# Relative values of an attention kernel: four query shifts with both halves of the table as weights, instead of eight shifts and three products

## The reference

```python
rel_pos = jnp.arange(L)[None, :] - jnp.arange(L)[:, None] + (MAX_LEN - 1)
rel_v = relative_v[rel_pos]                      # (L, L, 16): a row of the table for each pair
scores = jnp.einsum('bhld,bhrd->bhlr', Q, K) * scale + jnp.einsum('bhld,lrd->bhlr', Q, rel_k)
attn = jax.nn.softmax(scores, axis=-1)
out = jnp.einsum('bhlr,bhrd->bhld', attn, V) + jnp.einsum('bhlr,lrd->bhld', attn, rel_v)
```

## Time and profile before

| | us |
|---|---|
| median of three runs | 3464.99 (3463.78 to 3466.43) |
| span of the profiled execution, first to last instruction | 3463.7 |
| attention stage, about | 180 to 2890 |
| TensorE matmuls busy | 3194.2 (92%) |
| TensorE weight loads busy | 2524.8 (73%) |
| VectorE busy | 2813.3 (81%) |
| ScalarE busy | 2634.6 (76%) |
| GpSimd busy | 2262.5 (65%) |

### The profile page before, as it was taken

The page is one execution under the profiler, slowest core; times in us unless marked ns, Lnnn a source line. Parts: engine busy times, 40 slices in busy tenths (PEclk is TensorE's granted clock), DMA queues, the critical chain, the costliest instruction groups (busy, mean ns, idle before and its releaser), DMA issues. The chain is left out here.

```text
span 3463.7 us, 165894 instructions
## 1 busy us (share of the span) xinstructions
PE 3194.2 (92%) x64918; PEld 2524.8 (73%) x64918; DVE 2813.3 (81%) x7853; ACT 2634.6 (76%) x5852; POOL 2262.5 (65%) x2526
## 2 busy tenths in 40 slices
PE   7589999999999999999999999999999996999990
PEld 4357777777777777777777777777777785579980
DVE  6479999999999999999999999999999986534443
ACT  3288888888888888888888888888888893234440
POOL 0167777777777777777777777777777774700006
PEclk9779999999999999999999999999999997589995
DMA  7776666666666666666666666666666664712224
GB/s 212 228 230 216 221 220 221 221 221 224 218 221 224 221 223 224 222 218 224 221 223 224 223 217 221 224 224 221 224 218 222 222 217 161 239 51 69 62 62 145
DMA packets 356374, 701.28 MB, mean 202 GB/s; under 512 B 59545, under 2 KB 168706, under 8 KB 355346
## 3 DMA queue, kind: packets, MB, share of 16 engines
q1 hardware_dynamic: 349458, 673.92, 60.3%
q0 software_dynamic: 6144, 16.79, 1.5%
HBM read 343.02 MB, written 347.46 MB: 199 GB/s over the span
## 5 line engine op out<-in xcount | busy, mean ns | idle before, releaser
L850 POOL TENSOR_TENSOR pt_near<-pt_full,pt_near 128x512 f16<-128x512 f32 (+3 forms) x1984 | 1857.7, 965 | 583.8 <-DVE pt_near L1170 583.8
L1077 ACT ACTIVATE pt_full<-pb,exp_bias 128x512 f32<-128x512 f32 x2048 | 1313.5, 688 | 305.7 <-PE pb L960 183.9
L1011 PEld LDWEIGHTS pb<-pt_near,table_high 128*128 128x128 f16 x18432 | 794.6, 97 | 145.1 <-issue 106.4
L1011 PE MATMUL pb<-pt_near,table_high 128*128 128x64 f16 (+6 forms) x18432 | 884.8, 187 | 15.7 <-DVE rel_out L1203 14.6
L1150 DVE TENSOR_REDUCE part_max<-pb 128x1 f32<-128x512 f32 (+3 forms) x1376 | 771.2, 574 | 131.0 <-PE pb L918 130.0
L1011 PE MATMUL pb<-pt_near,table_low 128*128 128x64 f16 (+6 forms) x9216 | 851.4, 187 | 0.0
L1011 PEld LDWEIGHTS pb<-pt_near,table_low 128*128 128x128 f16 x9216 | 772.7, 97 | 0.0
L1146 DVE CUSTOM_DVE_ANT_0 near_sum<-pb,skewed 128x512 bf16<-128x512 f32 (+3 forms) x1216 | 675.6, 571 | 109.4 <-PE pb L918 85.0
L952 PE MATMUL pb<-ident,skewed 128*128 128x128 f32 x3840 | 621.6, 285 | 20.5 <-ACT q_max L1101 19.2
L1170 DVE CAST pt_near<-pt_full 128x512 f16<-128x512 f32 (+3 forms) x1280 | 532.3, 466 | 0.3 <-PE pb L984 0.3
L984 PE MATMUL pb<-v_head,pt_near 128*128 128x33 f16 x13440 | 507.2, 178 | 9.1 <-POOL pt_near L850 5.5
(11 more groups left out here) (182 smaller groups left out, 4063.3 us busy)
## 6 DMA issues: line engine op xcount, KB each, us to landing
skewed<-rel_scratch SPq DMA_DIRECT2D x256, 576.0 KB, 5.3
rel_scratch<-rel SPq DMA_DIRECT2D x416, 319.5 KB, 3.4
rel_scratch<-rel SPq DMA_DIRECT2D x320, 320.0 KB, 2.8
skewed<-rel_scratch SPq DMA_DIRECT2D x64, 512.0 KB, 4.6
skewed<-rel_scratch SPq DMA_DIRECT2D x64, 448.0 KB, 4.3
k_stack<-planes_scratch SPq DMA_DIRECT2D x192, 96.0 KB, 4.7
planes_scratch<-planes SPq DMA_DIRECT2D x64, 256.0 KB, 2.3
rel_scratch<-rel SPq DMA_DIRECT2D x64, 256.0 KB, 2.7
```

The lines of the kernel that those rows point to most:

```text
L850: ins = nc.gpsimd.tensor_tensor(pt_piece(c, 1, a, z, near), pt_full[e][:, (a - 4 * g) * P:(z - 4 * g) * P], pt_piece(c, 0, a, z, near), AL ...
L1011: ins = nc.tensor.matmul(acc[:, c0:c1, :], keep[table][:, w:w + P], pt_near[half][:, part, c0:c1, d - M_LO, a * SHIFTS:(a + 1) * SHIFTS], ...
L1077: nc.scalar.activation(pt_full[e][:, :], x_ps[e % 2][:, :], ACT.Exp, bias=exp_bias[:, 0:1]).then_inc(s_exp, 1)
```

## The change

The two halves of the table become weights side by side. A shift now takes 32 columns of the weights (16 of the high table, 16 of the low one), so 4 shifts fit (SHIFTS = 4), and there are 32 groups of 4 queries. The moving operand holds high and low probabilities of the group's 4 queries in 8 blocks, again 64 columns. One matmul makes all four products; low by low is new. A half head takes 32 x 9 = 288 matmuls, 36 a step. High and low probabilities end in different columns of the PSUM bank, so a half fills the bank four times instead of two, and each filling is emptied in two instructions: ScalarE copies the part of the low probabilities (128x256) to the chip's memory, VectorE adds the part of the high ones. GpSimd then masks, twice a half head, 128x512 each. In their engines' steps the copy (`take_low`) stands between the first two exponentials and the maximum's rows, the sum (`join_values`) behind the first two searches of the scores (the masking before stood at the step's beginning), and the mask between the three low parts and the output. The pick waits for the mask and comes one step later (LAG_SEL), and with it the sum over shifts and the output. TensorE's step holds no relative values in its middle when it begins a filling, which is now every second step. The table lies in HBM with high and low beside each other, and is loaded in two transfers of twice the size instead of four.

```diff
-SHIFTS = P // DK
+PARTS = 2
+PART_D = PARTS * DK
+SHIFTS = P // PART_D
 SHIFT_GROUPS = P // SHIFTS
+BANK_GROUPS = CH // (PARTS * HALF_C * SHIFTS)
+FLUSHES = SHIFT_GROUPS // BANK_GROUPS
+FLUSH_STEPS = HALF_C // FLUSHES
...
-LAG_SEL = LAG_RV + HALF_C
+LAG_SEL = LAG_RV + HALF_C + 1
...
+            def mask_values(it, h, part):
+                pool.wait_ge(s_rle, FLUSHES * h + FLUSHES // 2 * (part + 1))
+                pool.nop(nofuse=True)
+                half_a = SHIFT_GROUPS // 2
+                vals = rel_out[:, :, part * half_a:(part + 1) * half_a, :]
+                mask = keep["shift_mask"][:, :].rearrange("p (x y b) -> p x y b", x=1, y=1)
+                nc.gpsimd.tensor_tensor(vals, vals, mask.to_broadcast([P, HALF_C, half_a, SHIFTS]), ALU.mult).then_inc(s_rlm, 1)
...
+                for part in range(2):
+                    h, j = half_at(k, LAG_RV + HALF_C // 2 * (part + 1))
+                    if j == 0 and h >= 0 and exists(it, h * HALF_C):
+                        mask_values(it, h, part)
...
-                if quarter == 0 and j % 4 == 0:
+                if quarter == 0 and j % FLUSH_STEPS == 0:
                     if h or j:
-                        pe.wait_ge(s_rle, it * (2 * HALF_STEP) + 2 * h + j // 4)
+                        pe.wait_ge(s_rle, FLUSHES * h + j // FLUSH_STEPS)
...
                 for d in ds:
                     c0, c1 = half_range(half, d)
-                    for n, (table, part) in enumerate((("table_high", 0), ("table_high", 1), ("table_low", 0))):
-                        ins = nc.tensor.matmul(
-                            acc[:, c0:c1, :], keep[table][:, w:w + P],
-                            pt_near[half][:, part, c0:c1, d - M_LO, a * SHIFTS:(a + 1) * SHIFTS],
-                            start=(a % HALF_C == 0 and d == 0 and n == 0), stop=(a % HALF_C == HALF_C - 1 and d == M_LO and n == 2))
+                    ins = nc.tensor.matmul(
+                        acc[:, :, c0:c1, :], keep["table_pair"][:, w:w + P],
+                        pt_near[half][:, :, c0:c1, d - M_LO, a * SHIFTS:(a + 1) * SHIFTS],
+                        start=(g == 0 and d == ds[0]), stop=(g == BANK_GROUPS - 1 and d == ds[-1]))
...
-                    pe.wait_ge(s_rle, it * (2 * HALF_STEP) + 2 * h + 2)
+                    pe.wait_ge(s_rlm, 2 * h + 2)
-                first = 2 if rel_on and j else 0
+                first = 2 if rel_on and j % FLUSH_STEPS else 0
...
+            def take_low(it, h, f):
+                act.wait_ge(s_rl, FLUSHES * h + f + 1)
+                src = r_ps[:, :].rearrange("p (a r x) -> p r a x", r=PARTS, x=HALF_C * SHIFTS)[:, 1, :, :]
+                nc.scalar.copy(rel_low[:, :, :], src).then_inc(s_rlc, 1)
...
+            def join_values(it, h, f):
+                dve.wait_ge(s_rlc, FLUSHES * h + f + 1)
+                if f == 0 and h:
+                    dve.wait_ge(s_sel, PICK_BANKS * h)
+                dst = rel_out[:, :, f * BANK_GROUPS:(f + 1) * BANK_GROUPS, :].rearrange("p c a b -> p a c b")
+                src = r_ps[:, :].rearrange("p (a r c b) -> p r a c b", r=PARTS, c=HALF_C, b=SHIFTS)[:, 0, :, :, :]
+                low = rel_low[:, :, :].rearrange("p a (c b) -> p a c b", c=HALF_C)
+                nc.vector.tensor_tensor(dst, src, low, ALU.add).then_inc(s_rle, 1)
```

More of the change, by code:

```diff
@@ L332, in step @@
                     sp.nop(nofuse=True)
[L333 to L337, removed]
+                    for a, n, col in ((LEFT0, LEFT_N, 0), (MAIN0, MAIN_N, LEFT_N)):
+                        src = bass.AP(hbm["table"].tensor, (a - LEFT0) * PART_D, [[PART_D, P], [1, n * PART_D]])
+                        sp.dma_start(keep["table_pair"][:, col * PART_D:(col + n) * PART_D], src).then_inc(s_tbr, 16)
                     sp.wait_ge(s_rkp, 2)
@@ L442, in relative_values @@
             def relative_values():
[L443 removed]
+                rows = table[:, :].rearrange("p (n d) -> p n d", d=DK)
+                nc.vector.tensor_copy(table_parts[:, :, 0, :], rows).then_inc(s_tb, 1)
                 dve.wait_ge(s_tb, 1)
[L445 removed]
+                nc.vector.tensor_tensor(table_parts[:, :, 1, :], rows, table_parts[:, :, 0, :],
                                         ALU.subtract).then_inc(s_tb, 1)
@@ L1109, in step @@
                     exponentials(it, k - LAG_X, 1)
+                for f in range(FLUSHES):
+                    h, j = half_at(k, LAG_RV + FLUSH_STEPS * (f + 1))
+                    if j == 0 and h >= 0 and exists(it, h * HALF_C):
+                        take_low(it, h, f)
                 if exists(it, k - LAG_A):
@@ L1209, in sum_values @@
                     dve.wait_ge(s_o, it * HALF_STEP + h - 1)
-                src = bank_of("pick", h * HALF_C, n)[:, :].rearrange("p (c s d) -> p c d s", c=PICK_C, s=SHIFTS)
+                src = bank_of("pick", h * HALF_C, n)[:, :].rearrange("p (c s d) -> p c d s", c=PICK_C, d=DK)
                 nc.vector.tensor_reduce(rel_sum[h % 2][:, PICK_C * n:PICK_C * (n + 1), :], src,
@@ L1241, in step @@
                     search_bank(it, a, 2)
+                for f in range(FLUSHES):
+                    h, j = half_at(k, LAG_RV + FLUSH_STEPS * (f + 1))
+                    if j == 0 and h >= 0 and exists(it, h * HALF_C):
+                        join_values(it, h, f)
                 if exists(it, k - LAG_PV):
@@ L1846, in program @@
             keep["rk_stack"] = sbi("rk_stack", [P, RELN // 2], FP16)
-            keep["table_high"] = sbi("table_high", [P, TABLE_N * DK], FP16)
-            keep["table_low"] = sbi("table_low", [P, TABLE_N * DK], FP16)
+            keep["table_pair"] = sbi("table_pair", [P, TABLE_N * PART_D], FP16)
             keep["blank"] = sbi("blank", [CLEAR, D])
```

49 lines of the change are left out of this document (18 added, 31 removed).

## The result

The changed kernel takes 3550.26 us (median of four runs, 3549.62 to 3552.47), the kernel before 3465.71 (median of four runs, 3463.78 to 3468.21): a ratio of 1.0245, 95% interval 1.0232 to 1.0259. The forecast was 3449, faster, with a range of 3390 to 3505, so sign and range are both wrong.

What follows compares the result with a forecast made beforehand. TensorE was taken to bind in some 56 of 84 us a head, ScalarE close behind; -0.4 - 1.3 + 0.9 + 0.3 = -0.5 us a head, x 32 = -16 us, gave 3449 us, range 3390 to 3505.

Steps and rivals of the forecast that it cites:

- Prices: Forecast time of each new instruction: ScalarE's copy 0.35 us, VectorE's join 0.418, GpSimd's mask 1.25.
- TensorE's saving of work: Relative-value matmuls fall from 54 to 36 a query block, 8.6 us less weight loading a head, 274 over all.
- Rival 4: Relative-value matmuls on TensorE become slower; at double, 59.4 ns each, +6.8 us a head, 3683 us; chance 0.07.
- The reason given for the rate to stay: On TensorE, 128x128 weight loads pace matmuls of 16 and 64 columns alike, 54 in 1.53 us.
- the three masks outside the crowd: GpSimd masks in blocks 0 to 3 and 9 to 15 fit into its pauses, 0.1 us each, 0.3 a head.
- rival 1: Masks outside blocks 4 to 8 lengthen VectorE's two casts, 0.66 us each mask; +1.2 a head, 3503 us; chance 0.25.
- long casts in all blocks: Sign that masks meet VectorE's casts: long in every block; before, 420 ns in blocks 0 to 3, 751 in 4 to 8.
- Blocks 4 to 8: GpSimd has no gap there; the 1.25 us mask lengthens them, less 0.35 of ScalarE's wait: 0.9 us loss a head.
- The gains: Blocks 0 to 3 get 0.4 us shorter and blocks 9 to 15 1.3 us shorter, 1.7 a head.
- the waits left over: ScalarE's waits remaining after the change: 0.55 us in blocks 0 to 3, 1.0 in blocks 9 to 15.
- The join's wait: VectorE's join waits for ScalarE's copy; costed at nothing, since two bank searches cover it; uncovered, 2.8 us a head.
- the sums one block later: VectorE's two sums over shifts move one block later; costed at nothing, given 4.3 us idle in blocks 9 to 15.

Runs made afterwards that it cites:

- e3_before_pool: The kernel before with one more GpSimd instruction of the mask's form, on unused memory, at the change's four mask steps a head: 3501.36 us.
- e2_two_products: The kernel before without the product of low table and high probabilities, 288 relative-value matmuls a half head for 432, nothing else moved: 3407.07 us.
- e1_no_mask: The changed kernel with GpSimd's masking left out, the pick waiting for the joins instead: 3424.69 us.
- e13_mask_between: The changed kernel with GpSimd's mask issued behind the block's first low half instead of its third: 3546.69 us.

## Why the prediction was wrong

- **Prices, and TensorE's saving of work: right, the mask's by luck** (1.04 us alone, 1.28 with its waits). Rival 4 is out: 31.3 ns a matmul, not 44 or more. The reason given for the rate to stay is only half right: in a row it is 30.4 ns from one start to the next with 64 columns and 25.0 with 16 to 32, so the loads alone don't set the pace. The Trainium skill, "PSUM — Partial Sum Buffer", section "Specifications (TRN2)", warned of patterns that are not contiguous; this trace shows nearly nothing of it, with outputs in two pieces of a bank where a block has fewer than eight rows.
- **The step that failed: the three masks outside the crowd.** "They fit, but barely ... I take 0.1 each, 0.3". Measured against the kernel without a mask: 0.84 (block 2), 0.73 (block 10), 0.70 (block 14), together 2.27. The mechanism was that of rival 1, GpSimd and VectorE taking turns, and its price of 0.66 was close; but its sign, long casts in all blocks, shows in block 2 alone, and in blocks 10 and 14 the low half pays. The estimate had the right row, a low half that took 0.2 more beside an output, and took over its price, though that instruction was 0.46 us long and the mask is 1.04. The other fault was to measure the pauses (1.4 us, 0.2 us of loss at the output) in a schedule that TensorE held open, and to use them for one that the change itself draws together. e3_before_pool shows that in the old schedule they would nearly have fitted (0.4 to 0.5 for the three).
- **Blocks 4 to 8: +0.9 forecast, +1.52 measured.** The mask costs 1.86 there (29.72 - 27.86), not 1.25. About 1.0 to 1.2 is the mask (with the preparation spread 27.57 - 26.41 = 1.16, or 0.95 in the 18 of 24 heads in which the clock stayed full); most of the rest can be the granted clock, for which the forecast had no term (last section).
- **The gains: 1.7 forecast; without a mask 0.12 in blocks 0 to 3 and 0.77 in 9 to 15.** The saving alone gives 0.41 and 0.86 (e2_two_products): most blocks still take near 5 us with a third less relative-value work on TensorE. ScalarE's busy time was foreseen, with two copies in blocks 0 to 3 and three in 9 to 15 (19.03 and 33.70, measured 19.06 and 33.88); the term that was too small is the waits left over, 0.55 and 1.0 for 0.82 and 1.41. The two stretches of e1_no_mask, columns as in the earlier trace rows:

```profile
1426.53:1446.41 19.88, 18.48 (x403) 13.88 (x400) 18.61 (x55) 19.06 (x44) 14.15 (x16) 1.00 0.70 229
...
1474.25:1509.54 35.29, 33.50 (x734) 25.67 (x732) 32.51 (x103) 33.88 (x81) 25.67 (x30) 1.00 0.57 190
```

- **The join's wait and the sums one block later, both costed at nothing:** the wait is 82 us of VectorE's idle time (40.5 without a mask), and copies and joins cost 70 us with the pick at its old place. The shift gives 52 of them back, a gain that was not seen. That the two together cost only 18 us is luck.

Added up, a head is off by 2.0 (masks) + 0.6 (crowd) + 0.8 (gains) = 3.4 us, and -0.5 + 3.4 = 2.9 for 2.80 measured.

## What to carry to other kernels

A pause in the trace belongs to the schedule that the busiest engine imposes: when a change relieves that engine, the pause shrinks, so an addition that is to hide in it has to be priced against the shorter one. Here GpSimd's instructions take turns with VectorE's casts and its low half, so work for either is to be put into one sum with the other, wherever in the block it is issued; only a piece short enough for the pause that is left is in part hidden (0.26 us shown of a 128x256 mask). And a wait that names an engine is to be followed back until something in it has grown: ScalarE's wait for TensorE began with a mask on GpSimd.

## What the runs showed of the hardware beyond that

The granted clock fell in the crowded stretch of the changed kernel, in all 24 heads looked at, and in none of the kernel before. Windows of one microsecond (columns as above):

```profile
1519.50:1520.50 1.00, 0.91 (x13) 0.74 (x15) 1.00 (x3) 1.00 (x3) 0.86 (x2) 1.00 0.94 350
1520.50:1521.50 1.00, 0.59 (x14) 0.22 (x8) 0.89 (x5) 0.08 (x1) 1.00 (x2) 1.00 1.06 188
1521.50:1522.50 1.00, 0.36 (x8) 0.26 (x8) 1.00 (x5) 0.41 (x1) 1.00 (x2) 1.00 0.94 380
1522.50:1523.50 1.00, 0.33 (x9) 0.33 (x10) 0.00 (x0) 0.57 (x2) 1.00 (x2) 1.00 0.82 289
...
1525.50:1526.50 1.00, 1.00 (x27) 1.00 (x24) 1.00 (x4) 1.00 (x4) 0.57 (x2) 0.50 0.41 151
1526.50:1527.50 1.00, 1.00 (x21) 1.00 (x19) 1.00 (x3) 0.96 (x2) 1.00 (x2) 0.50 1.03 394
...
1528.50:1529.50 1.00, 1.00 (x23) 0.70 (x23) 0.17 (x1) 0.54 (x1) 1.00 (x2) 1.00 0.84 327
```

TensorE, which waits for GpSimd's low halves here, is busy for 0.59, 0.36 and 0.33 us in three windows; then the clock stands at 0.50 (1.2 GHz) for some 3 us before it is back at 1.00 (2.4 GHz). What that costs can be read within one run: with the mask on VectorE the clock fell in 7 of 24 heads, and these take 29.11 us in blocks 4 to 8, the other 17 take 28.29. Up to block 6 the two groups take the same (17.8 us in blocks 4 to 6); in block 7, where the clock falls, it is 5.98 and 5.35. One head of each:

```profile
1394.59:1422.84 28.25, 25.17 (x504) 18.23 (x501) 26.60 (x72) 24.41 (x56) 26.08 (x31) 1.00 0.79 253
1479.84:1508.89 29.05, 26.15 (x503) 19.36 (x501) 26.23 (x72) 24.39 (x56) 26.09 (x31) 0.94 0.76 249
```

The price depends on what else is late: with the mask between the low halves (e13_mask_between) the 10 heads with a lower clock, most of it in block 6, took only 0.11 us longer than the other 14. In the changed kernel it falls mostly in block 7, and blocks 7 and 8 take 0.69 us more than without a mask, which speaks for the upper end but doesn't show it. How much of the changed kernel's 1.86 us in these blocks is the clock's is therefore only bounded, 0.1 to 0.8 us a head, 3 to 26 us in all.
